# Folding the first tail normalisation's scale and shift into ACT's eviction of the transposed rows

## The reference

```python
x = _L0_conv_ref(x, ...)                       # attention over pixels, added to x
t = _to_tokens(x)                              # 8 x 1024 tokens of 128 channels
t = t + _L1_attn_ref(_ln_t(t), ...)            # global + local attention, below
t = t + _L1_ffn_ref(_ln_t(t), ...)             # mixture of 8 experts
# end of _L1_attn_ref:
x = layer_norm(x + x_fused, gn_g, gn_b)                         # "u": first tail normalisation
x_ffn = silu(x @ ffn_w1.T + ffn_b1) @ ffn_w2.T + ffn_b2
x = layer_norm(x + x_ffn, fn_g, fn_b)                           # "v": second
```

## Time and profile before

| what | before |
|---|---|
| median of 3 runs | 1966.23 us (1964.11 to 1969.98) |
| profiled execution, its own time | 1971.81 us |
| its span in the trace | 1969.2 us |
| mean granted TensorE clock | 0.888 of full |
| busy: PE, DVE, ACT, POOL | 82%, 68%, 52%, 36% |

### The profile page before, as it was taken

How to read it: one execution, slowest core, us unless ns; L and a number is a source line. 1 busy time by engine, 2 the same in 40 slices (tenths; PEclk the granted TensorE clock), 3 DMA queues, 4 the chain that set the end, 5 groups by cost and what they waited for, 6 DMA issues and landing times.

```text
span 1969.2 us, 24543 instructions
## 1 busy us (share of the span) xinstructions
PE 1616.7 (82%) x8264; PEld 759.1 (39%) x8264; DVE 1334.0 (68%) x2698; ACT 1031.5 (52%) x1970; POOL 715.0 (36%) x1113
## 2 busy tenths in 40 slices
PE   5758889998998898979898996889788886339993
PEld 2513322533443253325433442344223322227772
DVE  4258868797789768976897697869698821116660
ACT  1311566477656655665575665656564663223431
POOL 3101301245215530553154315421453441436883
PEclk7765899999999899989998998999898968559995
DMA  5281241335053405241533244132414110023346
GB/s 169 73 152 45 81 102 48 80 128 117 19 125 98 95 13 135 94 95 28 155 95 59 44 141 103 38 44 97 106 66 87 44 38 2 1 81 74 74 55 184
DMA packets 125921, 161.66 MB, mean 82 GB/s; under 512 B 19116, under 2 KB 86449, under 8 KB 125798
## 3 DMA queue, kind: packets, MB, share of 16 engines
q1 hardware_dynamic: 109926, 148.61, 29.6%
q0 software_dynamic: 13568, 7.31, 2.8%
q10 hardware_dynamic: 2304, 4.20, 0.6%
HBM read 103.36 MB, written 58.52 MB: 82 GB/s over the span
## 4 chain that ended last, share of the span: by engine, by line
PE 45%; DVE 18%; POOL 11%; DMA 9%; ACT 7%; SPq 6%; issue 5%; POOLq 0%; DVEq 0%; ACTq 0%
PE bank L1280 8%; PE bank L1249 7%; PE bank L1268 7%; DVE gmax L1728 7%; POOL t_d L1117 6%; PE bank L1206 6%; PE bank L1317 3%; PE bank L1307 3%; PE bank L1127 2%; SPq L891 2%; ACT prob L1523 2%; DVE cmax L1666 2%; DMA k_stack<-parts_d 2%; DMA kv_d<-lqkv 2%; DMA q_stack<-gneg_rows 2%
## 5 line engine op out<-in xcount | busy, mean ns | idle before, releaser
L1523 ACT ACTIVATE prob<-bank 128x512 f32<-128x512 f32 x1024 | 573.4, 596 | 348.8 <-PE bank L1268 346.9
L1728 DVE TENSOR_REDUCE gmax<-bank 128x1 f32<-128x512 f32 x1024 | 653.9, 681 | 65.9 <-PE bank L1249 65.0
L1268 PE MATMUL bank<-q_stack,k_stack 99*128 99x512 bf16 x1024 | 390.4, 397 | 71.1 <-ACT prob L1523 33.8
L1249 PE MATMUL bank<-k_stack,q_stack 96*128 96x512 bf16 x1024 | 402.9, 402 | 55.8 <-DVE gmax L1728 27.5
L1280 PE MATMUL bank<-prob,v_tok 128*32 128x512 f32 x2048 | 282.7, 626 | 2.1 <-ACT prob L1523 2.1
L1062 POOL TENSOR_TENSOR lprod<-ql_tok,kv_win 128x640 f32<-128x640 f32 x64 | 102.2, 1618 | 371.1 <-DMA ql_tok<-ql_d 347.1
L1249 PEld LDWEIGHTS bank<-k_stack,q_stack 96*128 96x128 bf16 x1024 | 101.4, 99 | 316.1 <-DVE gmax L1728 206.3
L1268 PEld LDWEIGHTS bank<-q_stack,k_stack 99*128 99x128 bf16 x1024 | 100.4, 100 | 249.0 <-ACT prob L1523 158.4
L1069 POOL TENSOR_TENSOR lprod<-ls,kv_win 128x640 f32<-128x640 f32 x64 | 80.8, 1284 | 227.5 <-DVE ls L1783 227.1
L1027 POOL TENSOR_TENSOR mv<-stats 128x4 f32<-128x4 f32 x64 | 13.0, 203 | 393.5 <-DVE stats L1700 393.5
L1117 POOL DMA_INDIRECT t_d<-kv_win,token_e x80 | 130.0, 1625 | 53.1 <-DVE kv_win L1928 29.0
(11 more groups left out here) (215 smaller groups left out, 2458.3 us busy)
## 6 DMA issues: line engine op xcount, KB each, us to landing
kv_win<-kv_d SPq DMA_DIRECT2D x32, 1280.0 KB, 5.6
parts_d<-parts SPq DMA_DIRECT2D x16, 768.0 KB, 3.6
q_stack<-parts_d SPq DMA_DIRECT2D x96, 128.0 KB, 6.9
k_stack<-parts_d SPq DMA_DIRECT2D x96, 128.0 KB, 7.4
kv_d<-lqkv SPq DMA_DIRECT2D x64, 128.0 KB, 2.5
rows_d<-rows SPq DMA_DIRECT2D x10, 528.0 KB
cprob<-rows_d SPq DMA_DIRECT2D x8, 660.0 KB, 4.7
x_cm<-in_x_dram SPq DMA_DIRECT2D x8, 512.0 KB, 3.5
```

The costliest lines, as they stand in the source:

```text
L1249: mm(max_ps[max_bank(n)][:, :], q_stack[quad][0:KROWS, h, i * P:(i + 1) * P], k_stack[quad][0:KROWS, h, j * HN:(j + 1) * HN], start=True, ...
L1268: mm(score_ps[n % 2][:, :], k_stack[quad][0:KM, h, j * P:(j + 1) * P], q_stack[quad][0:KM, h, half * HN:(half + 1) * HN], start=True, stop ...
L1523: nc.scalar.activation(prob[:, g % 2, h, :], score_ps[n % 2][:, :], ACT.Exp).then_inc(exp_made, 1)
L1728: v.tensor_reduce(gmax[:, h, i, j:j + 1], max_ps[max_bank(n)][:, :], AX.X, ALU.max)\
```

## The change

ACT's eviction of the transposed rows now computes gn_g * row + gn_b, with two columns `gn_cols` as scale and bias: after the transposition channels lie on partitions. So PE transposes the normalised rows themselves, as soon as ACT has them (`normed`), and POOL's `norm_u` becomes `affine_u`: a_old = x1 * gn_g, then a_old += (gn_b + ffn_b2), the sum of the two rows being made once. The addition of `fn_b` moves from `norm_v` into `bias`, where POOL adds it to all of `t_old`. Two columns more are loaded at the start. The planner's table and dependencies follow. (Of the two `x1_channels` in the diff the first is PE's, the second ACT's.)

```diff
-    "bias": [("pool", 2.4, 0.2)],
+    "bias": [("pool", 4.9, 0.2)],
-    "norm_u": [("act", 1.6, 0.1), ("pool", 4.0, 0.1)],
-    "norm_v": [("act", 1.6, 0.1), ("pool", 4.0, 0.1)],
+    "norm_u": [("act", 1.6, 0.1)],
+    "affine_u": [("pool", 2.6, 0.1)],
+    "norm_v": [("act", 1.6, 0.1), ("pool", 2.6, 0.1)],
...
+            if name == "u":
+                s.add("tail", a, ("affine_u", h), (a, ("norm_u", h)))
...
-        s.add("tail", a, ("ffn2", h), (a, ("ffn1", 1, h)), banks=TAIL_PS)
+        s.add("tail", a, ("ffn2", h), (a, ("ffn1", 1, h)), (a, ("affine_u", h)), banks=TAIL_PS)
...
+            loads += [(gn_cols[:, k:k + 1], v.rearrange("(c a) -> c a", a=1)) for k, v in enumerate((gn_g, gn_b))]
...
             def bias(b):
                 after(pool, recalled, (b + 1) * 32)
+                if b == 0:
+                    pool.tensor_tensor(bc[:, BC["gn_b"], :], bc[:, BC["gn_b"], :], bc[:, BC["ffn_b2"], :], ALU.add)\
+                        .then_inc(rows_summed, 1)
                 pool.tensor_tensor(a_old[:, :, :], a_old[:, :, :], wide(BC["fus_b2"], NT), ALU.add)\
                     .then_inc(bias_added, 1)
+                pool.tensor_tensor(t_old[:, :, :], t_old[:, :, :], wide(fnb_bc[:, :], NT), ALU.add).then_inc(t_bias, 1)
...
-            def norm_u(b, h):
+            def affine_u(b, h):
                 t = slice(HT * h, HT * h + HT)
                 after(pool, normed, b * 6 + h + 1)
-                pool.tensor_tensor(x1[:, t, :], x1[:, t, :], wide(BC["gn_g"]), ALU.mult).then_inc(affine_step, 1)
-                after(pool, affine_step, b * 6 + h * 1 + 1)
-                pool.tensor_tensor(x1[:, t, :], x1[:, t, :], wide(BC["gn_b"]), ALU.add).then_inc(x1_made, 1)
-
-                after(pool, x1_made, b * 2 + h + 1)
                 tail_done(pool, b, ("fuse2", h))
-                pool.tensor_tensor(a_old[:, t, :], x1[:, t, :], wide(BC["ffn_b2"]), ALU.add).then_inc(x1_bias, 1)
+                pool.tensor_tensor(a_old[:, t, :], x1[:, t, :], wide(BC["gn_g"]), ALU.mult).then_inc(affine_step, 1)
+                after(pool, affine_step, b * 4 + h + 1)
+                after(pool, rows_summed, 1)
+                pool.tensor_tensor(a_old[:, t, :], a_old[:, t, :], wide(BC["gn_b"]), ALU.add).then_inc(x1_bias, 1)
 
             def norm_v(b, h):
...
-                pool.tensor_tensor(x1[:, t, :], x1[:, t, :], wide(fnb_bc[:, :]), ALU.add).then_inc(affine_step, 1)
-                after(pool, affine_step, b * 6 + 2 + 2 * h + 2)
+                after(pool, affine_step, b * 4 + 2 + h + 1)
+                after(pool, t_bias, b + 1)
                 pool.tensor_tensor(x1[:, t, :], x1[:, t, :], t_old[:, t, :], ALU.add).then_inc(t2_made, 1)
...
             def x1_channels(b, h):
                 tail_fill_at(b, ("x1_channels", h))
-                after(pe, x1_made, b * 2 + h + 1)
+                after(pe, normed, b * 6 + h + 1)
...
             def x1_channels(b, h):
                 tail_wait(b, ("x1_channels", h))
-                to(y_cm[:, 0, h * HN:(h + 1) * HN], tail_ps[:, :]).then_inc(tail_free, 1)
+                to(y_cm[:, 0, h * HN:(h + 1) * HN], tail_ps[:, :], scale=gn_cols[:, 0:1], bias=gn_cols[:, 1:2])\
+                    .then_inc(tail_free, 1)
```

More of the change, by code:

```diff
@@ L510, in hybrid_kernel @@
         fnb_bc = sb("fnb_bc", [P, C])
+        gn_cols = sb("gn_cols", [P, 2])
         x_cm = sb("x_cm", [P, N])
@@ L653, in hybrid_kernel @@
         affine_step = sem("affine_step")
-        x1_made = sem("x1_made")
+        rows_summed = sem("rows_summed")
+        t_bias = sem("t_bias")
         x1_bias = sem("x1_bias")
@@ L778, in hybrid_kernel @@
         FIRST_LOADS = 2 + 1 + 11 + 1
-        WEIGHT_LOADS = FIRST_LOADS + len(NAT) - FIRST + 3 + len(BC) - 1 + 2
+        WEIGHT_LOADS = FIRST_LOADS + len(NAT) - FIRST + 3 + len(BC) - 1 + 2 + 2
         block = ctx.enter_context(nc.Block())
@@ L1094, in norm_v @@
                 pool.tensor_tensor(x1[:, t, :], x1[:, t, :], wide(BC["fn_g"]), ALU.mult).then_inc(affine_step, 1)
-                after(pool, affine_step, b * 6 + 2 + 2 * h + 1)
-                pool.tensor_tensor(x1[:, t, :], x1[:, t, :], wide(fnb_bc[:, :]), ALU.add).then_inc(affine_step, 1)
-                after(pool, affine_step, b * 6 + 2 + 2 * h + 2)
+                after(pool, affine_step, b * 4 + 2 + h + 1)
+                after(pool, t_bias, b + 1)
                 pool.tensor_tensor(x1[:, t, :], x1[:, t, :], t_old[:, t, :], ALU.add).then_inc(t2_made, 1)
@@ L1108, in _ @@
             walk("pool", dict(stats_t=stats_t, local_dot=local_dot, local_sum=local_sum, bias=bias, stats_u=stats_u,
-                            norm_u=norm_u, stats_v=stats_v, norm_v=norm_v, stats_t2=stats_t2, route=route))
+                            affine_u=affine_u, stats_v=stats_v, norm_v=norm_v, stats_t2=stats_t2, route=route))
             pool.wait_ge(t2_out, B * 16)
```

## The result

The changed kernel takes 1979.41 us in the median (1973.38 to 1984.07, 6 executions), beside 1966.23 us for the kernel before in the same session, the median of five executions; a sixth took 7463 us and is left out. The ratio of the two kernels is 1.0064, with a 95% interval of 1.0034 to 1.0095. The changed kernel is slower by 13 us (7 to 19 by the interval), where 3.25 us less were forecast. The profiled execution shown here took 1973.38 us (span 1970.9), the shortest of its six, and that of before 1971.81, longer than its median: the two spans differ by 1.7 us only, so they locate things, but the size of the loss is read from the medians.

The account below looks back on a forecast made before the run. No single engine bounds it: PE and DVE work in the middle, the dependent chain in the last tail, SP's queue at the start. Terms -2.14 + 0.36 - 2.67 + 1.2 = -3.25 us take 1966.2 to 1963.0 us, range 1951 to 1973.

Parts of the forecast that it names:

- eviction of half 0 sooner: First normalisation, last tail: ACT's eviction of half 0 starts at 1680.76 instead of 1682.90, -2.14 us.
- eviction with two columns: Last tail: ACT's scaled eviction takes 0.78 us, 0.18 more than a plain copy, twice on the chain: +0.36 us.
- statistics of v sooner, both steps together: Last tail, first normalisation: -2.14 us for the earlier eviction and +0.36 us for scaling with two columns.
- second normalisation: Last tail: taking POOL's L1096 out of both halves of norm_v removes 1.33 and 1.34 us, -2.67 us on the chain.
- PE's idle time ahead of the transposition: Last tail: PE's idle time before transposing x shrinks from 10.65 to about 7 us.
- start: Start of the run: two column loads ahead of the parts_d store in SP's queue cost +1.2 us, bounds 0.96 to 1.74.
- last score to route: End of the run: the span from the last score to the route becomes shorter by 4.5 us.
- The sum as a whole: Whole kernel, order neutral: -2.14 + 0.36 - 2.67 + 1.2 = -3.25 us, bounds -3.7 to -2.7; chance 0.47.
- seven of eight tails give nothing directly: Tails before the last: PE and DVE hardly wait for the two sooner POOL results, so only about one tail gains.
- the new order: All five queues may be interleaved anew by the planner's changed times; counted as zero in the forecast.
- slower by order: Guard rows fall behind local or stack loads in SP's queue in one more batch: 2.3 to 14.85 us, chance 0.17.
- The clock rival: Last tail: with less PE idle time the clock stays at 2.4 GHz, ffn1 products save 5 us, about 1958; chance 0.05.

Follow-up runs that it names:

- the version that follows: New step functions in the order of before, the two column loads issued from ACT's queue, against the kernel before: 1958.38 us, ratio 0.9957.
- 3.9: New step functions with the planner's table of before, norm_u's planned POOL time nudged from 4.0 to 3.9 us: 1983.58 us, ratio 1.0091 to the kernel before.
- 4.0: New step functions with the planner's table and dependencies of before, norm_u's planned POOL time left at 4.0 us: 1961.50 us, ratio 0.9967 to the kernel before.

## Why the prediction was wrong

**The steps of the last tail were right.** One by one, from DVE's statistics of half 0 on:

| step | predicted | measured |
|---|---|---|
| eviction of half 0 sooner | -2.14 | -2.24 (11.06 to 8.82 behind the statistics) |
| eviction with two columns | 0.78 us | 0.76 and 0.78 us; median 772 ns, plain 597 |
| statistics of v sooner, both steps together | -1.78 | -1.88 (37.93 to 36.05) |
| second normalisation | -2.67 | -2.68 (15.04 to 12.36 from v's statistics to t2's of half 1) |
| PE's idle time ahead of the transposition | about 7 us | 6.67 us |
| start | +1.2 | +1.17 |
| last score to route | -4.5 | -7.0 (107.5 to 100.5) |

The steps repeat: of the twelve profiles with the new functions ten have 36.05 or 36.06 us between the two statistics, and all have 6.66 or 6.67 us of idle time ahead of the transposition. The last row is 2.5 us more than the steps; these lie ahead of the change, between the last score and the statistics of u (33.87 to 31.37 us), where PE's clock rises sooner in this execution: sixteen products of `fuse2` take 2.02 us twice, where they took 3.00 and 2.57. That part takes 30.5 to 36.4 us in the profiles with the new functions, and is luck. At the start the guard rows were issued 0.66 us later (48.45), not 1.1; their landing took 0.5 us longer, and so +1.17 came out.

**The sum as a whole came out short**, with the order kept. Without the loads at the start it comes to -2.14 + 0.36 - 2.67 = -4.45 us, and the version that is just this measured -9.8, between -4.7 and -12.0 by its interval, which just leaves the sum out. With the loads it is -6.5 where the sum said -3.25, which its interval holds. The traces point to the stretch ahead of the last tail, where the prediction had "seven of eight tails give nothing directly". The last copy of `o_raw`, before, then with the new functions in the old order, and in the version that follows:

```profile
1637.97 0.60 ACT L1427 ACTIVATE o_raw<-bank 128x512 f32<-128x512 f32 x1 [1.29 <-PE bank L1280]
...
1628.13 0.60 ACT L1431 ACTIVATE o_raw<-bank 128x512 f32<-128x512 f32 x1 [1.29 <-PE bank L1284]
...
1629.30 0.60 ACT L1431 ACTIVATE o_raw<-bank 128x512 f32<-128x512 f32 x1 [1.28 <-PE bank L1284]
```

That is 9.8 and 8.7 us sooner. The profiled execution of before is 3.7 us above its median, the second is 4 us below its own and the last at its own, so that some 2 and 5 us are left, an estimate from these numbers. PE's idle time is the same as before (353.9 and 350.1 us beside 352.5) and its busy time 15.7 and 11.4 us less, which again is the clock, in part that of the slow execution of before. What in the change does this, no run shows.

That the second column is not free on ACT was taken from one operand's 90 ns, twice; 772 - 597 = 175 ns for both. The Trainium skill (ScalarE: Activation LUTs, "What ACT_TABLE_LOAD costs") says about 93 ns for each pointer operand; the trace agrees, with 175 ns for two at this size.

**The step that failed** is the one under "the new order": "I count this as zero in the forecast". The order costs +17 to +18 us, more than five times the sum. The text saw the lever (all five queues interleaved anew) and set its centre at zero, as if a new order could as well be better. Eight other orders were run with the new functions: by the medians none was better than the old one, one was equal to it, and seven were 5 to 22 us slower (two of them by 5 us, which is within the spread).

**The rival "slower by order"** had the right side and the wrong mechanism. It let the guard rows decide and priced them at one wait, 2.3 to 14.85 us. These waits rose by 1.8 us, and taking 28 to 30 us of them away gave at most 3 us back in one order and cost 10 in the other. Its chance of 0.17, and 0.12 for slower, came from looking at one kind of wait as if that kind carried the path. What the runs showed in its place: a loss spread over the middle batches, part in idle time of PE (1 to 8 us in five profiles) and the larger part, but for one profile, in products that run at the lower clock (7 to 18 us).

**The clock rival** was looked for in the wrong place. It was to give 5 us in the last tail; what it moved is PE's busy time, most of it in the middle stretch, where the profile of before had 0.96 and nothing drew attention to it. The 7 to 18 us are counted from the new functions in the old order. Beside the profile of before, an execution with 0.888, the first profile of the changed kernel is 5.7 us less busy and 7.4 us more idle. In two executions (the changed kernel's second set, and guard rows sooner in the new order) the clock was up for part of the last tail (in the second set 0.60 and 0.74 in the two stretches of 10 us from 1700 on, where the first has 0.50 in both) and v's statistics came 2.4 to 2.8 us earlier still, but there the part ahead of u's statistics was 5 us longer.

**Open** stays which of the displaced steps do it. The new orders differ from the old in 600 to 1250 of PE's steps, the loss has no single place, and the pair 3.9 and 4.0 shows the composition of the loss, not its first cause. That idle time ahead of them causes the slow products is read from the timelines; no run forced it.

## What to carry to other kernels

When a change feeds other times to a planner, predict two things: the edit at a fixed order, and the redraw. Measure them apart by keeping the old table for the new code. Don't centre the redraw on zero: here 0.1 us in one planned time cost 22 us, and no redraw gained anything. Nor does a right sum for one stretch bound the whole: with the order kept the change gave, by the medians, about twice its sum. A long wait in the list of waits is not a price; ask what the waiting engine would wait for next. And where all engines do the same work in a longer span, take the difference of the busy times first: idle time and slower products are told apart by one subtraction. Do it for several profiles, as the split moves from one execution to the next.

## What the runs showed of the hardware

The mean granted clock differs between executions of one program, and the time with it. Of 27 executions of the kernel before, the shortest (1959.74 us) had 0.901, the highest clock of all, and the longest (1976.70) 0.886, with 0.885 as the lowest. The spread of 17 us is as large as the effect of the order itself, so that only medians over many executions tell one order from another.

A load of 128 packets of 4 bytes took SP as long to issue as one of 64 KB, 0.43 us each and 0.47 from one to the next, and its landing did not set the pace: the store behind two of them came 0.94 us later, the first scores 1.17, where a pace set by the landings would have given 1.74 by the prediction's estimate.
